# A graph network on one core: the rest behind every fourth gather becomes two fills of the small tile instead of three

## The chip, the cores and the metric

The kernel runs on one core of a Trainium2 chip. The metric is device time in microseconds (us), as the median of several runs. The engines are PE (TensorE), DVE (VectorE), ACT (ScalarE), POOL (GpSimd) and SP (SyncE); the last only issues transfers here.

## The reference, cut to what matters

A graph has 3125 nodes of 64 features and 103125 edges, sorted by their destination. `_layernorm`, then a two-part block (L0), then five message-passing layers (L1):

```
# L0: attention over edges (4 heads) and a two-hop mean
h = einsum('ni,hio->nho', x, W_att)
e = leaky_relu(<h[src], a_src> + <h[dst], a_dst>)
alpha = segment_softmax(e, dst)
local = segment_sum(alpha[:, :, None] * h[src], dst).mean(axis=1)
for _ in range(2):  g = segment_sum(g[src], dst) / deg
x = x + concat([local, g @ W_g + b_g]) @ W_w + b_w
# L1: five layers over x = relu(layernorm(x)), with edge features of 32
for l in range(5):
    h = leaky(x @ W1[l] + b1[l]) @ W2[l] + b2[l]
    e = leaky(edge_attr @ We1[l] + be1[l]) @ We2[l] + be2[l]
    agg = segment_sum(h[src] * e * dot_scale[l], dst)
    x = layernorm(x + agg * res_w[l]) * ln_g[l] + ln_b[l]
```

All is in float32. Each pass over the edges looks up one row of a table of nodes for every edge (`h[src]`), and adds up rows of equal destination.

## The kernel before, in words

The edges lie in 128 rows of T = 808, and are worked through in CH = 101 chunks of K = 8 columns; a column is 128 edges. There are seven passes over all chunks: the hop pass (table1, first hop and scores), the GAT pass (table2, attention and second hop), and one for each of the five layers, called GINE (tableh).

A row of the table comes to an edge in one of two ways. For some columns of a chunk PE looks it up: DVE and ACT make one-hot matrices of the source numbers (`one_hot` at L1769, `one_hot_act` at L1006 and L1010), and PE multiplies them with the table in 25 matmuls a column (`look_up`, L1368; in the hop pass L1184); a DVE reduction (L1809) adds the parts. In the layers these are 2, 3, 3, 3 columns of four successive chunks (KPE), in the hop pass 2 and 3 in turn, in the GAT pass none. For the other columns POOL issues one indirect DMA each (a gather of 128 rows, `gather_chunk`, L708), so 6, 5, 5, 5 gathers of a chunk in a layer, 6 and 5 in the hop pass, 8 in the GAT pass.

The gathers go to `gring`, a ring of SL = 4 slots, one slot a chunk. Before the gathers of chunk c POOL waits until chunk c - 4 has been used; in the layers that is the multiply by the edge features on DVE (L1815), in the hop pass the running sum (L1488) and ACT's copy (L894), in the GAT pass ACT's weighing (L919, L921) and DVE's (L1688). Behind L1815, DVE carries the sum in (L1821) and makes the running sums (L1832); ACT copies them (L991), and SP stores them. Behind the running sums of the GAT pass (L1704) SP stores rows of 1296 KB a chunk. The edge features for a layer come from PE (`second_half`, L1382) on top of a bias that ACT writes (L981).

At the end of a pass POOL gathers the sums of the 3125 nodes with 25 indirect DMAs in a row (`gather_nodes`, L715), and the nodes' part follows: norm, two matmuls, a new table, for which POOL waits before its next pass.

POOL's order is written out: for every gather but the first, when the count of gathers so far is a multiple of BURST = 4, it calls `pause()` first. A pause fills the tile `rest` (128 x 256 float32, L699) with zeros, REST = 3 times, and POOL waits behind each fill for its end. No other instruction reads `rest`. The count runs on over all seven passes; `gather_nodes` does not count and has no pause.

Of the kernel before, what the change touches and what calls it, by code (L numbers as in the profile page):

```python
# [38 lines left out]

ON_ACT = 4  # L40
BURST = 4
REST = 3
KPE = (2, 3, 3, 3)
KMAX = max(KPE)
WIDE = (sum(KPE[0:2]) * P, sum(KPE[2:4]) * P)
# [58 lines left out]
def build(nc, x, src, dst, attr, W_att, a_src, a_dst, W_g, b_g, W_w, b_w, W1, b1, W2, b2, We1, be1, We2, be2,  # L104
          res_w, dot_scale, ln_g, ln_b, out):
    ctx = ExitStack()
    with ctx:
# [542 lines left out]
        def _(pool):  # L650
# [45 lines left out]
            def pause():  # L696

                for _ in range(REST):
                    pool.memset(rest[:, :], 0.0).then_inc(rested, 1)  # L699
# [1237 lines left out]
```

## Time and profile before

| | us |
|---|---|
| three runs, median | 6974.49 (6972.13 to 6980.57) |
| the profiled execution | 6960.44 |
| its span, first to last instruction | 6958.6 |
| hop pass, POOL's first to last gather | 40 to 919.5 |
| GAT pass | 1008 to 2302 |
| the five layers' passes | 2441 to 3280, 3352 to 4187, 4258 to 5091, 5163 to 6002, 6073 to 6908 |

The rows come from one profiled execution. A group of instructions is given as: line, engine, operation, what it writes <- what it reads, count | busy us in all, mean ns of one | idle us of the engine just before them, with what ended that idle time. "issue" is a gap that ends by nothing the profile shows. An instruction's busy time includes whatever holds it up once it has started.

### The profile page before, as it was taken

What the parts mean: (1) busy time and instruction counts of PE and PEld (TensorE: products, weight loads), DVE (VectorE), ACT (ScalarE), POOL (GpSimd) and SP (SyncE); (2) the same over time, 40 slices, a digit from 0 to 9 for tenths busy, and PEclk for the clock granted to TensorE, in tenths of its full rate; (3) what the DMA queues carried; (4) which work ended last, traced back from release to release, by engine and by line L of the source; (5) the groups of instructions that cost most, each with busy time, mean ns of one, the idle gap of its engine ahead of it and who ended that gap; (6) DMA issues with size and microseconds to landing.
All of it is one profiled execution on the core that took longest, in us unless ns stands there. A gap on an engine that the chain in (4) does not pass through costs nothing.

```text
span 6958.6 us, 134654 instructions
## 1 busy us (share of the span) xinstructions
PE 5066.8 (73%) x48820; PEld 4673.8 (67%) x48820; DVE 5088.1 (73%) x12225; ACT 4002.8 (58%) x6886; POOL 5252.7 (75%) x7260
## 2 busy tenths in 40 slices
PE   7888833333333588887788887888878888788886
PEld 7777732222222488887788886888868888688886
DVE  8776666666666577777687776777767777677776
ACT  5666626555555256665466664666646666466664
POOL 6777777777777377777677776777767777677777
PEclk9999965555555699998899997999979999799998
DMA  4444427777777333333233332333323333233332
GB/s 110 109 108 109 108 64 242 242 242 239 238 240 239 118 90 94 97 99 87 75 95 94 100 96 65 98 98 97 93 68 96 96 97 96 65 96 97 96 97 75
DMA packets 509379, 828.59 MB, mean 119 GB/s; under 512 B 112942, under 2 KB 220069, under 8 KB 495662
## 3 DMA queue, kind: packets, MB, share of 16 engines
q1 hardware_dynamic: 373374, 650.98, 27.9%
q0 software_dynamic: 135344, 169.01, 13.5%
q8 instruction: 389, 6.37, 0.4%
q14 instruction: 272, 2.23, 0.1%
HBM read 385.16 MB, written 434.48 MB: 118 GB/s over the span
## 4 chain that ended last, share of the span: by engine, by line
POOL 26%; DVE 15%; issue 12%; PE 8%; DMA 3%; another core or an unknown queue 2%; ACT 1%; DVEq 0%; POOLq 0%; ACTq 0%
POOL gring L708 20%; PE psum L1368 6%; DVE arena L1769 6%; POOL rest L699 6%; DMA gring<-tableh,src_i 2%; DVE by_lane L1832 2%; DVE psum L1815 2%; DVE gring L1809 1%; DVE es_w L1769 1%; POOL agg L715 1%; DVE psum L1821 1%; PE psum L1382 0%; ACT gring L1006 0%; ACT gring L1010 0%
## 5 line engine op out<-in xcount | busy, mean ns | idle before, releaser
L708 POOL DMA_INDIRECT gring<-tableh,src_i x2652 | 2574.6, 971 | 921.3 <-issue 612.5
L1368 PE MATMUL psum<-penalty,arena 125*128 125x192 bf16 x24736 | 2418.7, 253 | 363.5 <-DVE gring L1769 150.6
L1368 PEld LDWEIGHTS psum<-penalty,arena 125*128 125x128 bf16 x24736 | 2149.2, 101 | 453.2 <-ACTq L1014 226.0
L1769 DVE TENSOR_SCALAR arena<-dst_f,node_id 125x640 bf16<-125x640 f16 x4556 | 1779.8, 437 | 0.1
L708 POOL DMA_INDIRECT gring<-table,src_i x1364 | 1384.1, 1015 | 441.0 <-issue 316.3
L699 POOL MEMSET rest<- 128x256 f32 x3009 | 1077.1, 358 | 200.8 <-DMA tableh<-arena 85.1
L981 ACT COPY psum<-diag 128x512 f32<-128x512 f32 x505 | 297.6, 590 | 1496.2 <-DVE psum L1815 856.4
L1815 DVE TENSOR_TENSOR psum<-psum,gring 128x512 f32<-128x512 f32 x505 | 349.5, 692 | 511.4 <-DMA gring<-tableh,src_i 395.3
L1145 PE MATMUL psum<-ident,by_lane 128*128 128x128 f32 x202 | 66.7, 434 | 878.4 <-DMA by_lane<-attr_last 772.1
L1382 PE MATMUL psum<-arena 128*128 128x128 f32 x4040 | 579.9, 287 | 165.5 <-issue 155.9
L1809 DVE TENSOR_REDUCE gring<-psum 128x128 f32<-128x384 f32 x505 | 352.1, 697 | 432.3 <-PE psum L1368 261.2
L1145 PEld LDWEIGHTS psum<-ident,by_lane 128*128 128x128 f32 x202 | 29.2, 203 | 939.0 <-issue 939.0
L919 ACT ACTIVATE arena<-gring,es_w 128x65 f32<-128x65 f32 x1616 | 398.4, 335 | 454.2 <-DMA gring<-table,src_i 448.9
L1382 PEld LDWEIGHTS psum<-arena 128*128 128x128 f32 x4040 | 512.0, 198 | 192.4 <-issue 191.0
L1832 DVE TENSOR_TENSOR_SCAN by_lane<-mask_x,psum 128x256 f32<-128x256 f32 x1010 | 631.1, 663 | 0.2
L991 ACT COPY run<-by_lane 128x512 f32<-128x512 f32 x505 | 565.9, 1121 | 103.7 <-DVE by_lane L1832 48.1
L1704 DVE SCALAR_TENSOR_TENSOR arena<-arena,mask 128x324 f32<-128x324 f32 x808 | 443.3, 549 | 179.5 <-ACT arena L921 171.8
L1368 PE MATMUL psum<-penalty,gring 125*128 125x192 bf16 x3780 | 463.5, 254 | 21.2 <-issue 20.8
L1184 PE MATMUL psum<-x_nodes,arena 125*128 125x204 bf16 x3550 | 381.5, 265 | 115.3 <-DVE arena L1509 64.9
L1184 PEld LDWEIGHTS psum<-x_nodes,arena 125*128 125x128 bf16 x3550 | 338.7, 103 | 152.9 <-issue 135.7
L1006 ACT ACTIVATE gring<-dst_f,minus_id 125x768 bf16<-125x768 f16 x500 | 439.3, 926 | 0.0
L1010 ACT ACTIVATE gring<-gring,ones 125x768 bf16<-125x768 bf16 x500 | 436.4, 920 | 0.0
(272 smaller groups left out, 8095.3 us busy)
## 6 DMA issues: line engine op xcount, KB each, us to landing
rows<-arena SPq DMA_DIRECT2D x101, 1296.0 KB
acts<-arena SPq DMA_DIRECT2D x505, 256.0 KB
arena<-acts SPq DMA_DIRECT2D x505, 256.0 KB
rowsg<-run SPq DMA_DIRECT2D x505, 256.0 KB
gring<-tableh,src_i POOLq DMA_INDIRECT x2652
dst_f<-pe_src SPq DMA_DIRECT2D x430, 93.8 KB
rows<-run SPq DMA_DIRECT2D x101, 256.0 KB
gring<-table,src_i POOLq DMA_INDIRECT x1364
```

The lines of the kernel that those rows point to most:

```text
L699: pool.memset(rest[:, :], 0.0).then_inc(rested, 1)
L708: pool.indirect_dma_start(ring[:, s, k, :], None, table, bass.IndirectOffsetOnAxis(ap=src_i[:, c * K + k:c * K + k + 1], axis=0))\
L991: copy(run1[:, s, :, :], run_t[:, n % 2, :, :].rearrange("p f k -> p k f")).then_inc(rows_ready, 1)
L1006: nc.scalar.activation(slices[d], src_row[b], ACT.Abs, bias=minus_id[:, NV + half * some + d:NV + half * some + d + 1]).then_inc(hot_abs, 1)
L1010: ins = nc.scalar.activation(slices[d], slices[d], ACT.Relu, scale=-1.0, bias=ones[0:NQ, 0:1])
L1184: ins = mm(found1(c)[:, m, :], hot1[c // 2 % 2 * NJ + j][:, at:at + P], parts1[:, j, :, :].rearrange("q a w -> q (a w)"), start=(j == 0), ...
L1368: ins = mm(found(n)[:, m, :], hot_at(n // 2, j)[:, at:at + P], parts[:, j, :, :].rearrange("q a f -> q (a f)"), start=(j == 0), stop=(j == ...
L1382: ins = mm(o, act_in[:, n % SL, at:at + P], cur[:, :], start=False, stop=(u == 3), skip_group_check=True)
L1704: stt(run2[:, s % 2, k, :], prev, mask[:, bass.ds(c * K + k, 1)], msg2[:, s % 2, k, :], ALU.mult, ALU.add).then_inc(gat_steps, 1)
L1769: ins = ts(hot_at(pair, j), src_row[b], node_id[:, j:j + 1], None, ALU.is_equal)
L1815: tt(msgg(n).rearrange("p f k -> p k f"), psum[:, 2 + b, :].rearrange("p (k f) -> p k f", f=F), gatherg[:, s, :, :], ALU.mult).then_inc(ed ...
L1832: nc.vector.tensor_tensor_scan(run_t[:, b, half, :].rearrange("p f k -> p (f k)"), mask_x[:, b, half, :].rearrange("p f k -> p (f k)"), ms ...
```

## The change

One constant: the number of fills in a pause. It holds for all passes.

```
--- before.py
+++ after.py
@@ -39,7 +39,7 @@
 
 ON_ACT = 4
 BURST = 4
-REST = 3
+REST = 2
 KPE = (2, 3, 3, 3)
```

The places of the pauses stay, between the same gathers.

## Rows read from the trace of the kernel before

**Rows 1.** The page: busy shares; chain by engine, by line; POOL's fills

```profile
PE 5066.8 (73%) x48820; PEld 4673.8 (67%) x48820; DVE 5088.1 (73%) x12225; ACT 4002.8 (58%) x6886; POOL 5252.7 (75%) x7260
...
POOL 26%; DVE 15%; issue 12%; PE 8%; DMA 3%; another core or an unknown queue 2%; ACT 1%; DVEq 0%; POOLq 0%; ACTq 0%
POOL gring L708 20%; PE psum L1368 6%; DVE arena L1769 6%; POOL rest L699 6%; DMA gring<-tableh,src_i 2%; DVE by_lane L1832 2%; DVE psum L1815 2%; DVE gring L1809 1%; DVE es_w L1769 1%; POOL agg L715 1%; DVE psum L1821 1%; PE psum L1382 0%; ACT gring L1006 0%; ACT gring L1010 0%
...
L699 POOL MEMSET rest<- 128x256 f32 x3009 | 1077.1, 358 | 200.8 <-DMA tableh<-arena 85.1
```

**Rows 2.** Groups of POOL's instructions, hop pass, 40 to 919.5 us

```profile
L708 POOL DMA_INDIRECT gring<-table,src_i x556 | 547.2, 984 | 198.3 <-issue 128.9 <-POOL rest L699 35.2 <-DMA table<-arena 32.0
L699 POOL MEMSET rest<- 128x256 f32 x414 | 150.0, 362 | 15.9
```

**Rows 3.** The same view, GAT pass, 1007.7 to 2302.2 us

```profile
L708 POOL DMA_INDIRECT gring<-table,src_i x808 | 836.9, 1036 | 242.7 <-issue 187.5 <-POOL rest L699 52.8 <-ACT arena L921 1.4
L699 POOL MEMSET rest<- 128x256 f32 x606 | 192.2, 317 | 23.3
```

**Rows 4.** The same view, first layer, 2441 to 3280 us

```profile
L708 POOL DMA_INDIRECT gring<-tableh,src_i x531 | 515.3, 970 | 161.4 <-issue 122.7 <-POOL rest L699 36.4 <-DVE by_lane L1832 0.9
L699 POOL MEMSET rest<- 128x256 f32 x396 | 147.5, 372 | 15.2
```

**Rows 5.** The same view, last layer, 6073 to 6908.2 us

```profile
L699 POOL MEMSET rest<- 128x256 f32 x396 | 146.9, 371 | 15.2
```

**Rows 6.** Timeline of POOL in a layer: start us, us, instruction, [idle before]

```profile
4004.30 1.02 POOL L708 DMA_INDIRECT gring<-tableh,src_i  x1 [0.27 <-POOL rest L699]
4005.62 1.02 POOL L708 DMA_INDIRECT gring<-tableh,src_i  x1 [0.30 <-issue]
```

**Rows 7.** Waits of POOL, whole run: us in total, times, longest us

```profile
POOL gring L708 <- DVE psum L1815: 3.8, 14, 0.3
```

**Rows 8.** Waits of all engines, GAT pass, 1100 to 2290 us

```profile
ACT arena L919 <- DMA gring<-table,src_i: 430.7, 92, 7.1
DVE arena L1688 <- DMA gring<-table,src_i: 244.5, 91, 5.1
```

**Rows 9.** Waits, hop pass, 60 to 900 us

```profile
DVE run L1488 <- DMA gring<-table,src_i: 119.3, 38, 6.1
```

**Rows 10.** Waits, first layer, 2460 to 3270 us

```profile
DVE psum L1815 <- DMA gring<-tableh,src_i: 84.1, 38, 4.8
DVE gring L1809 <- PE psum L1368: 52.3, 23, 4.4
...
PE psum L1382 <- issue: 38.8, 24, 3.8
...
PE psum L1368 <- issue: 22.6, 39, 1.6
PE psum L1368 <- ACTq L1014: 14.1, 9, 3.1
```

**Rows 11.** Busy time by stretch: stretch, length, busy of each, clock, DMA share, GB/s

```profile
60.00:900.00 840.00, 718.49 (x6805) 663.04 (x6803) 633.36 (x2097) 534.05 (x879) 665.63 (x928) 0.95 0.42 109
1100.00:2290.00 1190.00, 398.97 (x1682) 262.90 (x1684) 750.71 (x1502) 680.92 (x2065) 943.17 (x1312) 0.58 0.72 240
2460.00:3270.00 810.00, 698.19 (x7492) 670.89 (x7490) 637.25 (x1517) 514.52 (x685) 639.44 (x897) 0.94 0.36 96
```

**Rows 12.** The page: DVE's one-hot instructions

```profile
L1769 DVE TENSOR_SCALAR arena<-dst_f,node_id 125x640 bf16<-125x640 f16 x4556 | 1779.8, 437 | 0.1
```

**Rows 13.** The line of one-hots: duration ns min/median/max, first and last start

```profile
L1769 DVE TENSOR_SCALAR arena<-dst_f,node_id x4556: 350/405/946, 2416.7 to 6898.9; 125x640 bf16<-125x640 f16 x110, 125x768 bf16<-125x768 f16 x89
```

**Rows 14.** The line of the nodes' gathers, same columns

```profile
L715 POOL DMA_INDIRECT agg<-rowsg,last_i x125: 938/944/1538, 3289.6 to 6946.8; - x125
```

**Rows 15.** Timeline of POOL, one of three such gathers in a row

```profile
1030.83 3.13 POOL L708 DMA_INDIRECT gring<-table,src_i  x1 [0.30 <-issue]
```

**Rows 16.** Timeline of DVE, one of five such instructions in a row

```profile
1029.62 3.52 DVE L1681 SCALAR_TENSOR_TENSOR es_w<-es_w 128x3232 f32<-128x3232 f32 x1
```

## The prediction

> **What bounds the kernel now.** I read the page's head first. POOL has the largest busy share, 75%, DVE and PE 73% each [rows 1], and the chain that ended last names POOL for 26%, the rests alone for 6% [rows 1]. Three busy shares that close settle nothing, and the mean covers seven edge passes and the pieces between them. So I took POOL's own instructions pass by pass. In the hop pass 556 gathers take 547.2 us, 414 fills 150.0 us, and the idle time in front of them is 198.3 + 15.9 us, of which 32.0 us is the wait for the table before the pass [rows 2]. That makes 547.2 + 150.0 + 166.3 + 15.9 = 879.4 us. The pass is 879.5 us long. The GAT pass: 836.9 + 192.2 + 242.7 + 23.3 = 1295.1 us, of a pass of 1294.5 [rows 3]. The first GINE layer: 515.3 + 147.5 + 161.4 + 15.2 = 839.4 us, of 839.0 [rows 4]. The four other layers repeat it; the last has 396 fills of 146.9 us again [rows 5]. So POOL's stream has no hole in any pass. What stands as idle is a fixed gap: 0.30 us between two gathers and 0.27 us behind a rest [rows 6].
>
> The waits say the same from the other side. Over the whole run POOL's gathers wait 3.8 us in 14 waits for the multiply that frees a ring slot in the layers (DVE L1815), none longer than 0.3 us [rows 7], and less in all for any other consumer. The ring of four slots is never full, hence consumers never set the pace, they follow it. They do wait for gathers: ACT 430.7 us in 92 waits in the GAT pass, DVE 244.5 us in 91 there, 119.3 us in the hop pass, 84.1 us in 38 waits in the first layer [rows 8 to 10].
>
> **The change, part by part.** Only the count of fills in a rest changes. No instruction of another engine, no DMA and no table is added or moved. The third fill and the wait on its own semaphore go, behind every fourth gather. There are 3009 fills [rows 1], so 1003 rests: 138 in the hop pass, 202 in the GAT pass, and the remaining 663 in the five layers.
>
> What one fill holds POOL for is its duration and the gap before it; the first fill of a rest starts at once behind the gather, so the idle time in front of the fills belongs to two of three.
> Hop: 150.0/414 = 0.362 and 15.9/276 = 0.058, together 0.420 us; times 138 = 58 us.
> GAT: 192.2/606 = 0.317 and 23.3/404 = 0.058, together 0.375 us; times 202 = 76 us.
> Layers: 147.5/396 = 0.372 and 15.2/264 = 0.058, together 0.430; the last layer has 0.371 and the three between lie a little lower, so I take 0.427 us; times 663 = 283 us.
> Sum 417 us. All of it lies on POOL's stream.
>
> What may come late next. Per chunk of eight columns (101 in a pass) POOL now takes 8.71 us in the hop pass, 12.82 in the GAT pass, 8.31 in a layer. With 1.37, 2.00 and 1.31 rests in a chunk it would take 8.14, 12.07 and 7.75. Against this stand the others' own needs in the inner stretch of each pass [rows 11]:
> In a layer PE is busy 698.19 of 810 us, so 7.16 us a chunk; DVE 637.25, so 6.54; ACT 514.52, so 5.28.
> In the hop pass PE 718.49 of 840 us, so 7.45 us a chunk; DVE 633.36, so 6.57.
> In the GAT pass DVE 750.71 of 1190 us, so 8.09; ACT 680.92, so 7.34; PE 4.3.
> All are below POOL's new time. PE in the layers is the nearest, 92% of 7.75. How near it really is I bound from both sides. From below: 7.16 us holds no wait at all, and the layer gets all of 283 us. From above: PE's waits there that name neither a gather nor DVE, issue 38.8 + 22.6 and ScalarE's sequencer 14.1 us [rows 10], are 0.77 us a chunk; if all of it stayed, PE's pace would be 7.93 and the layers would give (8.31 - 7.93) x 505 = 192 us, 91 less. I take the lower end and a quarter of the way up, 23 us lost, for two reasons. A late consumer costs nothing while a slot of the ring is free, and a slot is always free today. And DVE loses work by the change: its one-hot instructions have a median of 405 ns and a maximum of 946 where the mean over all 4556 is 437 [rows 12, 13], and POOL's fills are stretched in the layers (372 ns) and not in the GAT pass (317), which has no one-hots. The stretch is mutual, so fewer fills leave DVE some ns. I count that as nothing.
> The granted clock is 0.94 in the layers, where PE is busy for 86% of the time, and 0.58 in the GAT pass, where it is busy for 34% [rows 11]. A faster supply of gathers fills PE's gaps and should not lower it; I take no gain.
> In the GAT pass the DMA engines are busy for 72% and move 240 GB/s [rows 11]. The same bytes in 12.07 instead of 12.82 us a chunk are 255 GB/s and 76%. Below: nothing is lost. Above: the pass keeps its length and all of 76 us is lost. I take nothing lost, since no row shows an engine waiting for a store there, and ACT's 430.7 us of waits in 92 chunks (4.7 us each) are six times the 0.75 us that go.
> Behind the last gather of a pass the order of work is what it was, so the pieces between passes keep their length.
>
> A gather and DVE do disturb each other. In the stretch where DVE runs instructions of 3.52 us over 3232 elements, gathers behind it take 3.12 to 3.13 us, against 0.94 in quiet stretches [rows 14, 15, 16]. The Trainium skill, page "SBUF — State Buffer", section "Who interferes with whom", says that VectorE in a 2-port mode and GpSimd share one pair of ports, and the one that comes second is blocked for the whole of the other's instruction. By that rule gathers that follow a shorter rest would meet the same VectorE instructions and wait for them, and the removed fill could come back as blocked time; that is the third rival below. [...]
>
> The sum: the profiled execution took 6960.4 us; less 417, plus 23, is 6566 us. The median of the three runs, 6974.5, lies 14 us above the profiled execution. The forecast for the runs is 6580 us.
>
> **The rivals.**
> PE takes over. Its pace in the layers is 7.93 us, as worked out: 91 us fewer gained, 6960.4 - 417 + 91 + 14 = 6649 us. For it: PE's busy share of 86%, and DVE's waits for the look-up, 52.3 us in a layer [rows 10]. Against it: those waits occur while DVE blocks PE through its order.
> The GAT pass is held by transfers and gives nothing: 6544 + 76 + 14 = 6634 us. For it, 72% of the DMA engines; against it, the waits above.
> The time comes back in the gathers, by the ports: a gather is now 0.970 in the layers and 1.036 us in the GAT pass on average [rows 3, 4], against 0.94 quiet. If each of the 1003 rests gave back its 0.42 us the time stays at 6974 us. Against it: the disturbance in a layer is 0.03 us a gather today, and a fourteenfold of it would be needed in the one behind a rest.
> Slower: the rest lets the queue of gathers drain, and with two fills it does not drain in time; a gather then takes some 3.1 us instead of 0.95, as behind the long DVE work [rows 15]. The price is 2.2 us a gather; it decides from 417/2.2 = 190 of 4016 gathers, one in 21. At one in 16 it is 251 x 2.2 = 552 us, less 417: 135 us slower, 7110 us. For it: nothing else in the trace says what the rests are good for, and the trace can't show what happens at a denser issue in a pass. Against it: 25 gathers in a row without any rest (L715) have a median of 944 ns [rows 14], though beside little other work.
>
> **How the numbers follow.** Forecast (6530 to 6615): 0.60. PE takes over (6615 to 6710): 0.18. GAT pass held by transfers: 0.04. Back in the gathers, no change: 0.04. Slower: 0.14. About 0.2% is what a measurement of this kernel can tell from no change. Faster by more than that is 0.60 + 0.18 + 0.04 = 0.82, within it 0.04, slower 0.14. The range of 6530 to 6710 us takes in the full 417 us with 14 to spare (6544 + 14 = 6558, and the third fill may be the longest of the three) and PE's upper bound with some more; it leaves out 0.18.
>
> **What would show it.** POOL's fills x2006. The hop pass some 822 us long, the GAT pass 1219, each layer 783 to 790. The sum of POOL's busy time and fixed gaps equal to each pass's length shows that POOL still sets the pace; waits of POOL for L1815 or L1488 beyond 0.3 us would show that a consumer does. The mean of a gather up from 971 ns toward 1.05 us or beyond supports the third rival; many gathers of 2 us and more, the fourth. The prediction is wrong if the time is above 6710 us, and its reason is wrong if the layers shrink by less than 35 us each while the fills are gone.

## The result and the profile after

The changed kernel takes 7577.31 us (median of four runs, 7566.28 to 7594.39), the kernel before beside it 6977.53 us (6972.13 to 6981.87): a ratio of 1.0862, 95% interval 1.0837 to 1.0887. It is 600 us slower, where 6580 us was forecast. The same kernel, run again in two other jobs, takes 6509.0 and 6507.99 us against 6909.64 and 6905.40 (0.942 [0.9404, 0.9436] and 0.9422 [0.9404, 0.9441]): 400 us faster. Both are true, and most of what follows is about what tells the two apart. The unaltered change was slower in one job only: in the other jobs where the kernel before took as long as in this one, only relatives of it were run. One execution of a kernel below (two fills in the GAT pass alone) took 12600.41 us and is left out of its median.

The page of the changed kernel answers to [rows 1]:

```profile
PE 5559.2 (73%) x48815; PEld 4806.8 (64%) x48820; DVE 5000.5 (66%) x12225; ACT 4003.2 (53%) x6886; POOL 4899.2 (65%) x6257
...
PE 41%; DVE 12%; issue 10%; another core or an unknown queue 5%; ACT 1%; POOL 1%; DMA 0%; DVEq 0%; POOLq 0%; ACTq 0%
PE psum L1368 35%; PE psum L1382 5%; DVE arena L1769 5%; DVE by_lane L1832 2%; DVE psum L1815 1%; DVE es_w L1769 1%; POOL agg L715 1%; DVE gring L1809 0%; DVE psum L1821 0%; ACT gring L1006 0%; PE psum L1294 0%; PE psum L1325 0%; ACT gring L1010 0%; PE psum L1265 0%
...
L699 POOL MEMSET rest<- 128x256 f32 x2006 | 711.6, 355 | 417.3 <-DVE psum L1815 208.7
```

The fills are gone as they should, 2006 for 3009, and POOL is busy for 353.5 us less. But the chain of waits, which named POOL for 26%, names PE for 41%, its look-ups (L1368) for 35%. POOL's own groups pass by pass (columns as in [rows 2]) answer to [rows 2 to 4]: hop pass, 40 to 1035.3 us; GAT pass, 1141.5 to 2356; first layer, 2494 to 3430.2:

```profile
L708 POOL DMA_INDIRECT gring<-table,src_i x556 | 545.4, 981 | 312.0 <-issue 141.3 <-ACT es_w L894 79.5 <-DVE run L1488 39.7
L699 POOL MEMSET rest<- 128x256 f32 x276 | 97.2, 352 | 72.7 <-ACT es_w L894 37.1 <-DVE run L1488 26.9 <-issue 0.6
...
L708 POOL DMA_INDIRECT gring<-table,src_i x808 | 831.2, 1029 | 242.6 <-issue 217.4 <-ACT arena L921 16.0 <-POOL rest L699 8.9
L699 POOL MEMSET rest<- 128x256 f32 x403 | 129.6, 322 | 11.7
...
L708 POOL DMA_INDIRECT gring<-tableh,src_i x531 | 519.9, 979 | 267.4 <-issue 135.9 <-DVE psum L1815 111.1 <-POOL rest L699 20.1
L699 POOL MEMSET rest<- 128x256 f32 x265 | 97.4, 368 | 51.6 <-DVE psum L1815 43.8
```

The gathers are as long as before (979 for 970 ns in the layer, 981 for 984 in the hop pass, 1029 for 1036 in the GAT pass). The GAT pass, 1213.5 us from first to last gather, is what was forecast (1219). In the hop pass (994.8 us, before 879.0) and the layers (935.3, 930.4, 925.4, 934.9, 930.2; before 838.6 to 833.3) POOL now waits for the instruction that frees a slot. Over the whole run, against 3.8 us in [rows 7]:

```profile
POOL gring L708 <- DVE psum L1815: 578.3, 192, 7.3
POOL rest L699 <- DVE psum L1815: 208.7, 64, 8.3
```

L1815 in turn is late because of PE: the reduction L1809 that stands before it needs PE's look-ups. PE's waits in the first layer, 2513 to 3400 us, answer to [rows 10]; the windows over hop pass, GAT pass and layer answer to [rows 11]:

```profile
PE psum L1368 <- issue: 120.8, 262, 2.0
PE psum L1382 <- issue: 7.9, 21, 0.9
PE psum L1368 <- ACTq L1014: 2.5, 2, 1.4
PE psum L1368 <- DVE gring L1769: 2.4, 2, 2.0
```

```profile
60.00:1020.00 960.00, 796.69 (x6634) 666.26 (x6632) 613.35 (x2064) 521.95 (x858) 614.60 (x798) 0.88 0.36 94
1142.00:2355.00 1213.00, 424.40 (x1816) 282.32 (x1816) 825.66 (x1610) 731.21 (x2205) 958.96 (x1210) 0.60 0.75 252
2513.00:3400.00 887.00, 747.61 (x7181) 665.44 (x7180) 594.26 (x1444) 489.17 (x651) 581.58 (x750) 0.89 0.32 84
```

PE nearly stopped waiting for DVE's one-hots (2.4 us, before 31.4 in the same view). It has gaps inside its look-ups which end by nothing that the profile shows, 120.8 us in 262 gaps, where before it had 22.6 us in 39 [rows 10]. The granted clock went from 0.94 to 0.89, and from 0.95 to 0.88 in the hop pass; PE's busy time rose with it although its work is the same (747.61 us for 7181 matmuls, 104 ns each, against 698.19 for 7492, 93 ns). The clock is not the whole of this: at 93 ns for 0.94, a clock of 0.89 alone would give 98 ns, by our estimate. Broken stretches are longer in themselves: the eight matmuls at 4336.42 us below are busy for 1.15 us, 144 ns each, the unbroken sixteen at 4338.97 for 1.48 us, 92 ns each. One layer's timeline shows what the gaps go with (start us, us, instruction, [idle before]; some lines between 4332 and 4342 us):

```profile
4332.05 0.24 PE L1368 MATMUL psum<-penalty,gring 125*128 125x192 bf16 x1 [0.21 <-issue]
...
4335.68 0.50 PE L1368 MATMUL psum<-penalty,arena 125*128 125x192 bf16 x4 [0.47 <-issue]
...
4336.42 1.15 PE L1368 MATMUL psum<-penalty,arena 125*128 125x192 bf16 x8 [0.24 <-issue]
...
4336.90 0.94 POOL L708 DMA_INDIRECT gring<-tableh,src_i  x1 [0.31 <-issue]
...
4338.64 0.50 PE L1368 MATMUL psum<-penalty,gring 125*128 125x192 bf16 x4 [0.31 <-issue]
...
4338.74 0.76 DVE L1809 TENSOR_REDUCE gring<-psum 128x192 f32<-128x576 f32 x1 [8.65 <-remote]
...
4338.97 1.48 PE L1368 MATMUL psum<-penalty,arena 125*128 125x192 bf16 x16
...
4340.29 0.49 PE L1368 MATMUL psum<-penalty,es_w 125*128 125x192 bf16 x4
...
4341.04 1.48 PE L1368 MATMUL psum<-penalty,arena 125*128 125x192 bf16 x16
...
4341.77 1.14 POOL L708 DMA_INDIRECT gring<-tableh,src_i  x1 [3.93 <-DVE psum L1815]
```

While POOL gathers, PE stops every few matmuls. From 4337.84 us POOL stands still for 3.93 us, as its ring is full. PE still stops 0.8 us later (0.31 us before 4338.64), and from 4338.97 on it runs its matmuls without a gap, sixteen in 1.48 us, 92 ns each. The ring fills because its consumers are late, POOL then waits, and that wait stands in for the rest which the change took away: the loss limits itself.

PE's disturbance lags behind the gathers, and much of it falls into the rests themselves. A count of look-up time over the five layers (PE's busy time in L1368 and the gaps before it, by what POOL does at that moment) gives these shares lost to gaps: in the kernel before 2.0% beside gathers (53.5 of 2701 us) and 10.8% in rests (89.5 of 825 us); in the changed kernel 12% beside gathers, 31% in rests, and 9% while POOL stands for more than 0.45 us.

The timeline shows a second delay, which the gaps don't contain. The reduction L1809 at 4338.74 waits for the end of a look-up whose last matmul is the one at 4332.05, over by 4332.29 us; PE has gone on to other work since. DVE has stood idle for 8.65 us. The wait is put down to "remote", a queue that the profile doesn't know, but in the kernel L1809 waits there for one semaphore, `found_ps`, which only the look-up raises, and its rise is recorded at 4338.645 us. So PE's signal reached DVE 6.4 us after the look-up was done. Such waits in the first layer, before (2460 to 3270 us) and after (2513 to 3400 us):

```profile
DVE gring L1809 <- remote: 12.1, 8, 2.6
...
DVE gring L1809 <- remote: 166.0, 37, 18.3
```

Paired with its look-up, each of the 505 reductions of a run shows how long DVE stood idle although the look-up was over: 174 us in all in the kernel before, 799 us in the changed kernel. The pairing goes by the order of the instructions, because the traces hold fewer rises of that semaphore than look-ups (467 and 486 for 505).

Where the 609 us of the span went: hop pass +115.8, GAT pass -79.6, five layers +477.1 (the five differences above), the pieces between passes +96. Those between layers are 86 to 90 us long for 71 to 72 before: DVE's last multiply of a pass begins 16 to 21 us behind the end of the last gather, before 2 to 3 us, since the ring is full then.

### The profile page after: what moved, and what is told of

Same layout as the page of the kernel before. It is cut to its first block, busy times and chain, and to the rows that moved or that the text cites. A ratio compares the mean times of both kernels' runs of the same rounds, so it can differ in the third digit from the quotient of the medians.

```text
span 7568.0 us, 133646 instructions
## 1 busy us (share of the span) xinstructions
PE 5559.2 (73%) x48815; PEld 4806.8 (64%) x48820; DVE 5000.5 (66%) x12225; ACT 4003.2 (53%) x6886; POOL 4899.2 (65%) x6257
## 4 chain that ended last, share of the span: by engine, by line
PE 41%; DVE 12%; issue 10%; another core or an unknown queue 5%; ACT 1%; POOL 1%; DMA 0%; DVEq 0%; POOLq 0%; ACTq 0%
PE psum L1368 35%; PE psum L1382 5%; DVE arena L1769 5%; DVE by_lane L1832 2%; DVE psum L1815 1%; DVE es_w L1769 1%; POOL agg L715 1%; DVE gring L1809 0%; DVE psum L1821 0%; ACT gring L1006 0%; PE psum L1294 0%; PE psum L1325 0%; ACT gring L1010 0%; PE psum L1265 0%
## 5 line engine op out<-in xcount | busy, mean ns | idle before, releaser
L1368 PE MATMUL psum<-penalty,arena 125*128 125x192 bf16 x24736 | 2662.0, 258 | 482.6 <-issue 439.2
L1368 PEld LDWEIGHTS psum<-penalty,arena 125*128 125x128 bf16 x24736 | 2198.6, 103 | 761.8 <-issue 693.0
L708 POOL DMA_INDIRECT gring<-table,src_i x1364 | 1376.6, 1009 | 554.6 <-issue 358.7
L1769 DVE TENSOR_SCALAR arena<-dst_f,node_id 125x640 bf16<-125x640 f16 x4556 | 1726.7, 426 | 0.6 <-DMA dst_f<-pe_src 0.4
L1809 DVE TENSOR_REDUCE gring<-psum 128x128 f32<-128x384 f32 x505 | 355.2, 703 | 1576.6 <-remote 1019.6
L699 POOL MEMSET rest<- 128x256 f32 x2006 | 711.6, 355 | 417.3 <-DVE psum L1815 208.7
L1382 PE MATMUL psum<-arena 128*128 128x128 f32 x4040 | 650.0, 302 | 73.1 <-issue 59.6
L1382 PEld LDWEIGHTS psum<-arena 128*128 128x128 f32 x4040 | 567.4, 211 | 109.3 <-issue 106.9
L1368 PE MATMUL psum<-penalty,gring 125*128 125x192 bf16 x3780 | 504.7, 263 | 61.4 <-issue 59.1
L1184 PE MATMUL psum<-x_nodes,arena 125*128 125x204 bf16 x3550 | 427.6, 271 | 95.6 <-issue 92.6
L1368 PE MATMUL psum<-penalty,es_w 125*128 125x192 bf16 x3024 | 427.0, 262 | 58.3 <-issue 57.3
L1368 PE MATMUL psum<-penalty,xin 125*128 125x192 bf16 x3160 | 407.7, 255 | 60.1 <-issue 58.6
```

The costliest lines, as they stand in the source:

```text
L708: pool.indirect_dma_start(ring[:, s, k, :], None, table, bass.IndirectOffsetOnAxis(ap=src_i[:, c * K + k:c * K + k + 1], axis=0))\
L1184: ins = mm(found1(c)[:, m, :], hot1[c // 2 % 2 * NJ + j][:, at:at + P], parts1[:, j, :, :].rearrange("q a w -> q (a w)"), start=(j == 0), ...
L1368: ins = mm(found(n)[:, m, :], hot_at(n // 2, j)[:, at:at + P], parts[:, j, :, :].rearrange("q a f -> q (a f)"), start=(j == 0), stop=(j == ...
L1382: ins = mm(o, act_in[:, n % SL, at:at + P], cur[:, :], start=False, stop=(u == 3), skip_group_check=True)
L1769: ins = ts(hot_at(pair, j), src_row[b], node_id[:, j:j + 1], None, ALU.is_equal)
L1809: nc.vector.tensor_reduce(gatherg[:, s, K - kp(n):, :], found(n).rearrange("p m (a f) -> p m f a", a=3), AX.X, ALU.add).then_inc(edge_step ...
```

## The experiments

Eighteen runs in six jobs; all kernels of a job ran beside the kernel before. What the kernel before took tells the jobs apart. In three it took 6906, 6910 and 6905 us ("6908 jobs"), in three more and in the job of the result 6975, 6975, 6982 and 6978 us ("6975 jobs"). The expectations say "kind of chip"; the record doesn't bear that out, as chip number 15 stands beside one job of each kind (the numbers don't name the machine). In all tables, a layer's length is the mean of the five passes from first to last gather.

### The change and its parts where the kernel before takes 6906 us

**GAT pass alone with two fills**, the kernel before with one more parameter through `gather_chunk` and `pause` (cut to two places, "..." between them):

```
 REST = 3
+REST_GAT = 2
...
-                gather_chunk(c, c % SL, table2, gather2, g2_ready, K)
+                gather_chunk(c, c % SL, table2, gather2, g2_ready, K, REST_GAT)
```

> Two fills in the GAT pass alone, three in the hop pass and the layers. Theory A (supply): a burst of four gathers starves PE of instructions, PE stands within a look-up with gaps that nothing in the trace ends, and the time from the last gather of a burst to the first of the next is what lets the supply catch up. The GAT pass asks little of PE, so it gains its 1295 - 1213 = 80 us there, and hop pass and layers stay at 879 and 836 us: about 6978 - 80 = 6898 us. Theory B (the lost time is spread, any pass with two fills loses): the same kernel would be at 6978 or above.

Measured: 6818.23 us, 0.9868 [0.9848, 0.9888]; GAT pass 1208.4 us, the layers 835.8 as before. The 76 us of the GAT pass are there, and a little more.

**Two long fills**, together about as long as three:

```
-                    pool.memset(rest[:, :], 0.0).then_inc(rested, 1)
+                    pool.memset(rest[:, :].bitcast(BF16)[:, 0:464], 0.0).then_inc(rested, 1)
```

> Two fills everywhere, but each over 464 elements (bf16, in the same tile) instead of 256. If a fill costs about the same per element, the rest is as long as with three fills (about 1.05 us of fills, 1.34 us from gather to gather). Theory A (length of the rest decides): about 6975 us, layers at some 836 us. Theory C (the count of fills, or of their waits, decides): about 7577 us, layers at some 930 us.

Measured: 6841.25 us, 0.9905 [0.9885, 0.9925]; layers 828.3. Both theories had started from 6977 us, so neither number is met.

**Three short fills**, REST = 3 and `rest` of 128 columns:

> Three fills everywhere, each over 128 elements instead of 256: fills of 128 took 205 ns where fills of 256 took 312, so the fills of a rest take about 0.73 us, against 0.69 with two of 256 and 1.06 with three. Theory A (length decides): 7450 to 7600 us, PE's gaps within look-ups as after the change. Theory C (count decides): the rest is 0.33 us shorter without harm, 6977 - 0.33 x 1003 = 6650 us.

Measured: 6574.94 us, 0.9519 [0.95, 0.9538]; layers 789.9, hop 836.2.

**Half a look-up**, in the changed kernel:

```
-                        for j in range(NJ):
+                        for j in range(0, NJ, 2):
```

> The changed kernel (two fills), and in the layers a look-up has 13 of its 25 matmuls a column, so its sums leave out 12 of 25 groups of nodes; the hop pass is untouched. Theory A (PE's supply of instructions is what runs short): PE asks for some 45% fewer instructions in the layers, POOL sets the pace again at about 7.75 us a chunk, a layer takes some 785 us instead of 931, the hop pass stays at 995: 7577 - 5 x 146 = 6850 us. Theory D (DVE, ACT or the ring of slots holds the layers, PE's gaps are a by-product): layers stay above 880 us, 7320 us or more.

Measured: 6508.13 us, 0.9423 [0.9404, 0.9442]; layers 784.3. It had nothing to tell here: the hop pass, whose look-ups are whole, took 822.4 us with two fills, and none of the four kernels had a single gap that ends by nothing within the look-ups of the layers, nor a wait put down to "remote". The loss of the result did not exist in this job.

### The same two kernels again

**The changed kernel, unaltered:**

> The changed kernel once more, unaltered, since PE's gaps within look-ups were absent from the hop pass of a kernel whose hop pass is the same as its. Theory A (supply, and how short it is depends on the chip or on where the program lies there): on a chip where kernel before takes about 6906 us, POOL sets the pace and it takes what POOL's stream says, some 6906 - 417 = 6490 to 6570 us, with no gaps within look-ups; on a chip like the first one, about 7577. Theory E (the change is slower everywhere, by something that the half look-up took away): about 7500 us on any chip.

**The kernel before, unaltered, with a profile:**

> The kernel before, unaltered, with a profile, on the same chip as the run of the change. Theory A: if it takes about 6906 us its look-ups have no gaps at the end of a burst, where the first profile had PE idle for some 15% of the last microsecond before the next burst; if it takes about 6977 us they are there. Theory E: the gaps are the same in both.

Measured: 6509.0 us against 6909.64; the profiled execution of the kernel before took 6909.38. The windows of hop pass, GAT pass and first layer of the changed kernel, and PE's waits in that layer, columns as above:

```profile
60.00:860.00 800.00, 713.62 (x6904) 671.44 (x6902) 640.12 (x2133) 543.56 (x889) 630.30 (x811) 0.95 0.45 117
980.00:2190.00 1210.00, 436.94 (x1828) 287.50 (x1828) 813.49 (x1618) 735.48 (x2222) 939.32 (x1198) 0.58 0.76 254
2280.00:3065.00 785.00, 704.12 (x7729) 689.98 (x7730) 640.96 (x1545) 521.54 (x697) 615.56 (x792) 0.95 0.38 101
```

```profile
PE psum L1368 <- DVE gring L1769: 41.3, 22, 3.1
PE psum L1382 <- issue: 24.9, 15, 3.1
PE psum L1368 <- DVE xin L1769: 13.5, 13, 2.5
```

Hop pass 821.9, GAT 1212.5, layers 787.3, 783.2, 782.6, 786.4, 782.2 us: the forecast's 822, 1219 and 783 to 790. Here POOL still sets the pace in every pass. "PE L1368 <- issue" has no row at all, in this kernel or in the kernel before, and neither has "DVE L1809 <- remote": DVE stood idle behind finished look-ups for at most 1 us in all in either. The same holds for all ten traces of 6908 jobs, and all ten of 6975 jobs have both rows. The kernel before had the same pass lengths in both kinds of job (879.0 and 878.4, 1293.1 and 1296.5, layers 835.8 and 836.7): with three fills the difference lies outside the passes. The two profiled executions are 51 us apart, of which the pieces between the passes make 58 and the passes -7. One place shows it, the nodes' part between the first two layers. The kernel before in the job of the result, then the same lines in this job:

```profile
3314.91 0.37 ACT L956 COPY xT<-psum 128x250 f32<-128x250 f32 x1 [6.06 <-issue]
...
3318.68 0.94 POOL L715 DMA_INDIRECT agg<-rowsg,last_i  x1 [0.30 <-issue]
...
3324.74 0.49 DVE L1790 TENSOR_TENSOR arena<-psum,b_rows 125x320 f32<-125x320 f32 x1 [11.71 <-remote]
```

```profile
3293.48 0.37 ACT L956 COPY xT<-psum 128x250 f32<-128x250 f32 x1 [2.02 <-PE psum L1305]
...
3296.82 0.48 DVE L1790 TENSOR_TENSOR arena<-psum,b_rows 125x320 f32<-125x320 f32 x1
```

In the 6975 job DVE stands for 11.71 us, with PE's part of its input (L1325) done at 3312.2 us, and ACT for 6.06 us, while POOL issues 25 gathers in a row; the last of these ends at 3320.9 us and DVE goes on 3.8 us later. What DVE waits for is the semaphore that PE raises behind L1325, and its rise is recorded at 3324.72 us: again the signal is late, by 12.5 us, and not the work. In the 6908 job DVE doesn't stop and ACT stands for 2.02 us, beside the same 25 gathers. POOL's next pass therefore starts 62.2 us after the last gather of the pass before, not 72.4.

### Fewer fills where the kernel before takes 6975 us

REST = 1 and REST = 0 (the loop of `pause` then runs once or never):

> One fill in a rest, in all passes. If kernel before takes about 6906 us beside it (PE's supply is ample): POOL's stream is 2 x 417 us shorter than with three fills; in the layers it would be at 7.19 us a chunk, below PE's need of 7.16 plus its waits, so PE takes over there at 7.2 to 7.5: 6070 to 6230 us. If kernel before takes about 6977 us (supply short): theory A says it starves PE more than two fills, 7577 us or more; a theory in which only a rest of 0.97 us happens to fall badly says less than 7577.

> No rest at all. With an ample supply (kernel before at about 6906 us): POOL could do a chunk in 6.63 us in the layers and 10.6 in the GAT pass; the layers are PE's at 7.2 to 7.5 us, the hop pass PE's at 7.5 to 7.8, the GAT pass at 10.6 or held by transfers at 290 GB/s: 5950 to 6150 us. If PE's supply gives way on this chip too once gathers follow each other without a break (theory A), PE shows gaps within look-ups and the time is above that with one fill. With a short supply (6977 us beside it): above 7577.

Measured: 8057.71 us, 1.1554 [1.152, 1.1588], and 8191.74 us, 1.1746 [1.1624, 1.1868]. Both are far above the changed kernel. Each fill that goes adds to the loss, the later ones less (600, 480 and 134 us, across two jobs). PE's gaps over the whole run, of the kernel before, the changed one, one fill and none:

```profile
PE psum L1368 <- issue: 141.9, 247, 3.2
```

```profile
PE psum L1368 <- issue: 614.2, 1390, 2.0
```

```profile
PE psum L1368 <- issue: 853.3, 1512, 2.5
```

```profile
PE psum L1368 <- issue: 934.9, 1397, 3.2
```

The GAT pass, in which PE has little to do, took 1293.1, 1213.5, 1244.8 and 1287.3 us: two fills are best there.

### What the gaps depend on

Four kernels in one 6975 job. **Half a look-up**, as above:

> Two fills, and 13 of the 25 matmuls of each look-up in the five GINE layers (12 are left out, and with them part of the message). Where the kernel before takes about 6975 us (supply theory: bursts of gathers starve PE's instruction supply, and PE asks too much of it): PE needs about 38 matmuls less in a group of look-ups of 75, so with the same starving the layers have room again: 783 to 800 us each instead of 925 to 935, while the hop pass, whose look-ups are whole, stays at about 995 us with gaps that end by nothing inside its look-ups. Time about 7577 - 5 x 140 = 6880 us. Rival (POOL's own stream, or the DMA queue, is what got slow on such a chip): the layers stay at 920 us or more, about 7550 us. Where the kernel before takes about 6908 us, both give 6508 us again and tell nothing.

**Three short fills**, as above:

> Three fills of 128 columns instead of 256: the rest keeps its three instructions and loses 0.3 to 0.4 us of its length. Where the kernel before takes about 6975 us: if the length of the rest is what lets PE's supply catch up, this loses as the change does: 7450 to 7577 us, hop pass near 985, layers 915 to 930. If the number of POOL instructions in the rest matters (each one a chance for something else to pass), the passes shorten as their sum says: hop 836, layers 787 to 793, about 6640 us. Where the kernel before takes about 6908 us both give 6575 us.

**GAT pass alone**, as above:

> Two fills in the GAT pass alone, three elsewhere. PE is busy for a third of the GAT pass only, so it does not matter there how well it is supplied: the pass takes 1213 us instead of 1293 on either kind of chip, all others keep their length, 80 us less in all: about 6895 us where the kernel before takes 6975, about 6820 where it takes 6908. Rival: the loss of the whole change on the first chip spread from the GAT pass too (by what it leaves in queues): then 6975 or more.

**Narrow gathers** in the layers, two fills:

```
-                    pool.indirect_dma_start(ring[:, s, k, :], None, table,
+                    pool.indirect_dma_start(ring[:, s, k, 0:wide], None, table,
...
-                    gather_chunk(c, n % SL, tableh, gatherg, gg_ready, K - kp(n))
+                    gather_chunk(c, n % SL, ed_nodes, gatherg, gg_ready, K - kp(n), H)
```

> Two fills, and in the five layers a gather fetches 4 columns of a small table for each of its 128 rows in place of 64 of the large one (the message then multiplies what an earlier gather left, so the result of the layers is not the reference's). The number of gathers and descriptors is the same, the bytes a sixteenth. Where the kernel before takes about 6975 us: if the bytes that the gathers move slow the fetch of PE's instructions, the layers fall to 783 to 800 us and the run to about 6880. If it is the issue and the descriptors, of which there are as many, the layers stay at 920 to 935 and the run at about 7550. Where the kernel before takes about 6908 us both give about 6509.

| in this job (before 6975.48) | us | ratio | hop | GAT | layer |
|---|---|---|---|---|---|
| half a look-up | 6867.25 | 0.9837 [0.9786, 0.9889] | 949.9 | 1207.7 | 808.5 |
| three short fills | 7325.43 | 1.0509 [1.048, 1.0538] | 945.0 | 1235.3 | 889.3 |
| GAT alone | 6881.35 | 0.9862 [0.9842, 0.9881] | 879.1 | 1208.9 | 835.1 |
| narrow gathers | 7323.86 | 1.0499 [1.0461, 1.0537] | 953.4 | 1209.0 | 895.6 |

Halving PE's matmuls takes most of the loss out of the layers (808.5 us), and the hop pass of that kernel, with its whole look-ups, keeps it (949.9). So it is PE's side that holds the layers, and not POOL's own stream or its queue. It does not show what PE is short of, because the disturbance itself stayed: 524.7 us in 1011 gaps, one in 18 matmuls of the look-ups where the changed kernel has 614.2 us in 1390, one in 25, and DVE stood idle behind finished look-ups for 842 us. With half the work PE only has the time to bear it.

```profile
PE psum L1368 <- issue: 524.7, 1011, 3.0
```

The short fills say what of a rest counts. POOL stands for 1.09 us from gather to gather (median) in their rests, 1.06 in the changed kernel's, 1.52 in those of before. Three short fills lose like two whole ones: 945.0 us in the hop pass, against 949.9 and 953.4 of the two kernels with two whole fills in this job. The length counts and not the number of instructions. The expectation's 7450 was too high, perhaps because this job loses less than that of the result at an equal rest (953 for 995 us in the hop pass). POOL's groups in the second layer, narrow gathers first, then the whole ones behind short fills:

```profile
L708 POOL DMA_INDIRECT gring<-ed_nodes,src_i x530 | 519.0, 979 | 269.7 <-issue 134.1 <-DVE psum L1815 82.9 <-DMA tableh<-arena 31.3
```

```profile
L708 POOL DMA_INDIRECT gring<-tableh,src_i x530 | 518.4, 978 | 270.4 <-issue 131.2 <-DVE psum L1815 87.0 <-DMA tableh<-arena 31.4
```

POOL waits alike for L1815, the rests are alike, the bytes of a gather differ by a factor of sixteen, and the loss is the same. What disturbs PE is that gathers are issued, or their descriptors, not mainly what they move; the expectation for that case (layers of 920 to 935 us, 7550 us in all) was too high again. The unaltered change was not in this job, so small effects of either kind stay open.

### How the rest is divided

**The change again**, **bursts of two** (BURST = 2, REST = 1: as many fills, one behind every second gather), **two long fills** and **narrow gathers**, meant for a 6975 job, came to a 6908 job:

> The changed kernel, unaltered, as the measure for the three beside it. Where the kernel before takes about 6975 us: 7400 to 7580 us, hop pass 950 to 995, layers 885 to 935. Where it takes about 6908: 6509 us.

> One fill behind every second gather in place of two behind every fourth: the same number of fills in all, in shorter bursts. Where the kernel before takes about 6975 us: if a burst is what starves PE (its store of instructions lasts some 3 us into a burst in the kernel before), bursts of two gathers, 2.4 us, lose nothing and the time is some 6600 to 6700 us. If the share of time without a gather counts, it stays where the change is, 7400 to 7580. If a single fill is too short for PE's supply to get going at all, it goes toward the kernel with one fill, 8050. Where the kernel before takes 6908 us: about 6510 in all cases.

> Two fills in all passes, each long enough that the two last nearly as long as three of the kernel before. Where the kernel before takes about 6975 us: if the length of the rest counts, 6900 to 6990 us, the hop pass near 872, layers 830 to 838, no gaps in the look-ups. If the number of instructions in a rest counts, it loses as the change: 7400 or more. Where the kernel before takes 6908 us: 6841 again.

> Two fills, and gathers of 4 columns in place of 64 in the layers (a sixteenth of the bytes, the same number of gathers and descriptors; what the message reads there is then not the reference's). Where the kernel before takes about 6975 us: if bytes play no part, the layers are as long as those of the unaltered change beside it, within 10 us each; if they do, at least 30 us shorter each, so 150 us in all. Where it takes 6908 us: 6509 in both cases.

Measured: 6507.99, 6481.07 (0.9385 [0.9366, 0.9403]), 6849.43 (0.9922 [0.9902, 0.9941]) and 6506.66 us (0.9424 [0.9406, 0.9443]). None has a look-up gap that ends by nothing. Two of them were then run in one more job, which was a 6975 one:

> One fill behind every second gather. Where the kernel before takes about 6975 us: if a long unbroken burst is what starves PE, some 6550 to 6700 us; if the share of time without a gather counts, 7400 to 7580 as the change; if one fill alone is too short for anything, toward the 8050 of one fill behind every fourth. Where the kernel before takes 6908 us: 6481 again.

> Two fills that last nearly as long as the three of before. Where the kernel before takes about 6975 us: if the length of the rest counts, 6900 to 7050 us; if its number of instructions, 7400 or more. Where it takes 6908 us: 6845 again.

Measured: 7719.4 us, 1.1039 [1.0978, 1.1101], and 7050.14 us, 1.0097 [1.0078, 1.0117]. Bursts of two, the fastest kernel in the 6908 jobs, lose at least what the change lost in its own job (it was not run in this one). So breaking up the burst does not save PE: what counts is how little pause there is in all. The two long fills, whose rest of 1.38 us is nearly that of before, lose little; their gaps are many, but POOL waits for L1815 only 48.5 + 48.4 us:

```profile
PE psum L1368 <- issue: 477.0, 907, 3.1
```

```profile
POOL rest L699 <- DVE psum L1815: 48.5, 15, 3.5
POOL gring L708 <- DVE psum L1815: 48.4, 53, 3.3
```

In order of the pause for each gather, which is the median rest less the 0.30 us that two gathers have between them anyway, divided by the gathers of a burst (own count over the traces):

| 6975 jobs | pause a gather, us | layer, us | the same in a 6908 job |
|---|---|---|---|
| before | 0.30 | 835.8 | 836.7 |
| two long fills | 0.27 | 843.1 | 829.2 |
| three short fills | 0.20 | 889.3 | 789.9 |
| the change | 0.19 | 931.2 | 784.3 |
| bursts of two | 0.18 | 945.2 | 778.8 |
| one fill | 0.09 | 998.0 | not run |
| none | 0 | 1009.2 | not run |

In a 6908 job less pause is less time; in a 6975 job it is more, and the kernel before stands at the edge, with 3.8 us of POOL waiting. The first column is from four jobs, the second from three, and jobs of one kind differ among each other.

## Why the prediction was wrong

**What bounds the kernel: right.** POOL's stream did set the pace of all passes, and where it kept doing so the sum came out: 400.6 and 397.4 us gained, forecast 394 from median to median. There the 23 us that were taken off for PE were luck. The layers did give 262 us and not 283, but POOL's gathers waited for L1815 only 6.3 us in 23 waits, none longer than 0.3 us: the mean rest went from 1.50 to 1.10 us, so the third fill was worth 0.40 and not 0.427 us.

**The sum on POOL's stream: right.** The GAT pass came to 1213.5 us in the job of the result also; it gave 79.6 us, forecast 76. Transfers did not hold it: the DMA share rose from 0.72 to 0.75 and the rate from 240 to 252 GB/s. The second rival is false.

**"What may come late next": this step failed.** It took each engine's need from its busy time in the kernel before: PE 7.16 us a chunk, at most 7.93 with its unexplained waits kept as they were. Against that the changed kernel needed 935.3/101 = 9.26 us in the first layer. The waits that end by nothing were read as an amount which could only stay. They were what grew: from 22.6 us in 810 to 120.8 us in 887. Nor had the prediction a term for a finished look-up whose signal comes late, and that grew over the run from 174 to 799 us. The rests were costed as pure delay of POOL; in this kind of job they are also what lets PE and its signals come back in time. "A late consumer costs nothing while a slot of the ring is free" is true, but four slots only put it off: the consumers were late in chunk after chunk. The layers grew by 92 to 97 us each, where a shrinking of less than 35 us was named as the sign of a wrong reason.

**The granted clock: this held in one kind of job only.** It was not to fall. It stayed at 0.95 in the 6908 job, and fell from 0.94 to 0.89 in the job of the result.

**PE takes over (6649 us): right in kind, wrong in size.** A chunk's pace went to PE, but to a PE slowed by the very change. In the layer's window the gaps of the look-ups are 120.8 - 22.6 = 98 us more, and 7181 matmuls at 104 and not 93 ns, at the lower clock, 78 us more. Waits that went take back 29 us (for DVE's one-hots), 31 (L1382) and 12 (ACT's sequencer). That is 104 us; by its matmuls the window is 111 us too long (887 us for 7181, against 810 for 7492).

**Back in the gathers: false.** The mean of all gathers in the layers is 978 ns for 971. The text beside it, on ports that VectorE and POOL share, explained nothing of this result.

**The slower rival: right sign, wrong mechanism.** It had the gathers lengthen to some 3.1 us when their queue no longer drains; none in the layers took more than 1.74 us. What does not recover in time is on PE's side. For it the prediction wrote only that "nothing else in the trace says what the rests are good for". Two rows did: the 22.6 us that end by nothing inside PE's look-ups, and DVE's 12.1 us put down to "remote". Both rows are missing in the kernel before where the change pays. The share of look-up time lost to gaps, by the time since the first gather behind a rest, was in the first layer of the kernel before at most 2% up to 4.5 us, 6% from 4.5 to 5 us, 16% from 5.0 to 5.5 and 11% from 5.5 to 6.0, where POOL is already in its next rest, and 0 from 6.0 us on; in the changed kernel it was 6 to 28% up to 5 us, 33% from 5.0 to 5.5 and 44% from 5.5 to 6.0. That the disturbance builds up over a burst and ends in the rest was to be had from the trace ahead of the result.

**Shown and not shown.** Shown: gaps inside look-ups which end by nothing, only in 6975 jobs; they grow as the pause per gather shrinks, and the pass follows when they use up the slack; signals of PE that reach DVE after the look-up is over, in the same jobs only; halving PE's matmuls takes most of the loss away, though not the gaps; the bytes of the gathers matter little, and dividing the rest does not help. Argued only: that what PE lacks is its instructions. For it: the gaps lie between matmuls of one look-up, and no wait is named for them; within bad phases they come every four matmuls (the commonest distance, 313 of 1389 in the changed kernel), 0.36 us each in the median. Against it, or at least beside it: the semaphores' late rises, which a lack of PE's instructions doesn't explain once the matmuls have run, and the half look-up, which asks for half the matmuls and has more gaps for each. The 389 packets of 16 KB on the queue of instructions, one in some 126 matmuls, neither took longer (median 1.05 us, and 1.03 in the 6908 job) nor do the gaps keep to them. So if instructions are late it is not by the transfer of those packets. Open too are how the 600 us divide between the gaps and the late signals, whether both have one cause, and what makes a job one kind or the other.

## What to carry to other kernels

Before a pause is costed as dead time, look where between two pauses the other engines have gaps that end by nothing, and for waits put down to "remote" in a kernel on one core: compare the rise of the semaphore with the end of the work that it tells of. In this kernel gaps that grew toward the end of a burst and ended in the pause meant that the pause was used, and their sum was no bound for what they became. Where the kernel before takes one of two times from job to job, time a change to POOL's rhythm in both kinds: the same edit was worth -401 us and +600 us. Here two fills in the GAT pass alone are the version that beats the kernel before in both, by 88 and by 94 us (6818.23 against 6906.09, 6881.35 against 6975.48); two fills in all passes or bursts of two are right only where the 6908 us are sure.

## What was not expected of the hardware

- A stretch of indirect gathers from POOL goes with gaps in PE's stream of small matmuls for which the profile names no wait, in some jobs and not in others: 614.2 us of such gaps in one run, none in another of the same program. The kernel before shows the difference by 1% only.
- In the same jobs the signal that PE's work is done reaches DVE late: 6.4 us in the wait shown, 9.9 us at most and 799 us in all for the look-ups of the changed kernel, 174 us in the kernel before, and at most 1 us in either kernel in a 6908 job.
- The granted clock fell from 0.94 to 0.89 in a layer of the changed kernel, and its matmuls took 104 ns for 93. In the 6908 job the changed kernel, with PE busier (704.12 of 785 us), was granted 0.95. Gaps alone do not bring the clock down: the two long fills, with 477.0 us of them, were granted 0.98 from 2500 to 3280 us.
- A loss of this kind limits itself: late consumers let the ring fill, POOL waits, and these waits stand in for the rests. Even with no fill at all the layers ended at 1009 us, 11 us above one fill.
